# Scans with shifted dense rows and shared silu tables, an earlier spread of C, a router's logits moved up, and squares moved to GpSimd

## The reference, cut to what matters

```python
# grouped experts (layer 1, twice): 16 experts, the best 4 within 2 of 4 groups, two shared experts
scores = sigmoid(x @ router.T)          # the rest of the routing is left out
h = silu(x @ gate.T) * (x @ up.T)
y = combine(scores) * (h @ down.T)
...
# scans (layer 2): block a is one selective scan, block b is the difference of two
h_t = exp(delta_t * A) * h_(t-1) + (delta_t * u_t) * B_t     # 16 states for each of 256 inner features
y_t = sum over states of h_t * C_t, + D * u_t                # times silu(z), then a projection
delta = softplus(...);  u = silu(conv(...))
# the dense rows between and behind them (layer 2, twice)
h = silu(x @ w1 * s1) * (x @ w2 * s2)
h = gelu(h @ h1 * sh1);  h = gelu(h @ h2 * sh2);  y = h @ w3 * s3
...
# soft experts (layer 3, twice): 64 experts of 32 slots
D = softmax over slots (logits);  C = softmax over experts (logits)
X = tanh(layernorm(sum over tokens of D * x))
Y = X @ expert_w + expert_b
y = sum over experts and slots of C * Y
```

## Time and profile before

| | us |
|---|---|
| median of 3 runs | 3169.46 (3167.76 to 3170.31) |
| the profiled execution | 3163.47, of which its span 3161.8 |
| TensorE busy with products (PE) | 2879.4 (91% of the span) |
| TensorE loading weights (PEld, beside PE) | 1663.5 (53%) |
| VectorE busy (DVE) | 2187.7 (69%) |
| ScalarE busy (ACT) | 1641.4 (52%) |
| GpSimd busy (POOL) | 1119.3 (35%) |

### The profile page before, as it was taken

The page is one execution under the profiler, slowest core; times in us unless marked ns, Lnnn a source line. Parts: engine busy times, 40 slices in busy tenths (PEclk is TensorE's granted clock), DMA queues, the critical chain, the costliest instruction groups (busy, mean ns, idle before and its releaser), DMA issues. The chain is left out here.

```text
span 3161.8 us, 59104 instructions
## 1 busy us (share of the span) xinstructions
PE 2879.4 (91%) x22949; PEld 1663.5 (53%) x22949; DVE 2187.7 (69%) x4853; ACT 1641.4 (52%) x3287; POOL 1119.3 (35%) x534
## 2 busy tenths in 40 slices
PE   7888899998999999998968998898889899998999
PEld 3333344443899999643434544444454344574547
DVE  6777735556677777667588877877861559936991
ACT  3554543443333333326367776776753556725762
POOL 1111130002100000100088887877840209922990
PEclk8999999999555555699979999999999999999999
DMA  5344323022000000030532332222302001250225
GB/s 160 91 104 106 92 83 112 10 87 90 4 4 4 4 4 4 2 110 1 179 124 87 83 100 86 83 83 81 96 27 89 16 1 80 93 200 1 93 93 200
DMA packets 113494, 234.36 MB, mean 74 GB/s; under 512 B 13760, under 2 KB 50752, under 8 KB 104768
## 3 DMA queue, kind: packets, MB, share of 16 engines
q1 hardware_dynamic: 113216, 230.59, 22.7%
HBM read 185.71 MB, written 44.83 MB: 73 GB/s over the span
## 5 line engine op out<-in xcount | busy, mean ns | idle before, releaser
L2724 DVE TENSOR_TENSOR_SCAN s_hh<-psum,s_dbu 128x512 f32<-128x512 f32 x384 | 447.1, 1207 | 65.1 <-ACT psum L2337 62.4
L1447 PE MATMUL psum<-h_ring,h_parts 128*128 128x4 f16 x12264 | 478.3, 168 | 0.8 <-DVE h_ring L1590 0.6
L2594 POOL TENSOR_TENSOR s_dbu<-s_du,s_bb 128x1024 f32<-128x1024 f32 x191 | 446.7, 2362 | 60.9 <-DVE s_hh L2724 49.9
L1447 PEld LDWEIGHTS psum<-h_ring,h_parts 128*128 128x128 f16 x12264 | 430.5, 106 | 48.1 <-DVE h_ring L1590 0.8
L1509 ACT ACTIVATE h_now<-psum 128x16 f32<-128x16 f32 x1024 | 187.3, 183 | 325.5 <-PE psum L1447 319.0
L2337 ACT ACTIVATE psum<-s_delta,s_decay 128x512 f32<-128x512 f32 x384 | 256.4, 686 | 105.5 <-DVE s_hh L2724 103.4
L2229 PEld LDWEIGHTS psum<-w_c,s_term 128*128 128x128 f32 x1536 | 196.5, 148 | 129.5 <-issue 114.1
L1590 DVE TENSOR_SCALAR h_ring<-h_now 128x16 f16<-128x16 f32 x1024 | 179.3, 175 | 115.5 <-ACT h_now L1509 4.7
L1000 POOL MEMSET r_weights<- 128x512 f32 x4 | 2.1, 524 | 720.7 <-POOLq L1399 512.0
L2229 PE MATMUL psum<-w_c,s_term 128*128 128x128 f32 x1536 | 227.5, 284 | 6.7 <-ACT s_y L2415 6.2
L1592 DVE SCALAR_TENSOR_TENSOR h_ring<-h_now,h_ring 128x16 f16<-128x16 f32 x1024 | 181.2, 177 | 35.2
(11 more groups left out here) (585 smaller groups left out, 6257.9 us busy)
## 6 DMA issues: line engine op xcount, KB each, us to landing
s_bb<-s_wide SPq DMA_DIRECT2D x192, 256.0 KB, 3.5
x_spill<-x_flip SPq DMA_DIRECT2D x28, 1024.0 KB, 3.8
f_share<-f_wide SPq DMA_DIRECT2D x208, 128.0 KB, 3.0
s_cc<-s_wide SPq DMA_DIRECT2D x60, 256.0 KB, 3.4
a_ks<-a_spread SPq DMA_DIRECT2D x96, 128.0 KB, 3.4
a_qs<-a_spread SPq DMA_DIRECT2D x96, 128.0 KB, 3.9
x_spare<-x_spill SPq DMA_DIRECT2D x4, 2048.0 KB, 10.5
x_raw<-x_spill SPq DMA_DIRECT2D x4, 2048.0 KB, 9.3
```

Of the source, the lines that this page charges most:

```text
L1447: mm = nc.tensor.matmul(here[:, cols], parts[:, part, GROUP * grp + p, :], ring[:, (i - 1) % RING, grp, cut, cols], start=False, stop=True ...
L2594: nc.gpsimd.tensor_tensor(dbu[:, s % D_RING], du[:, t % 2], both(bb[:, s % B_RING, :]), ALU.mult).then_inc(dbu_ready, 1)
L2724: nc.vector.tensor_tensor_scan(hh[:, s % 4, half, :], DECAYS[i % 3], dbu[:, s % D_RING, half, :], 0.0, ALU.mult, ALU.add).then_inc(scan_do ...
```

## The change

1. Scans. Chunks 2 to 5 of the dense rows begin three or four slots later (`DENSE_AT`), and their pauses stand so that they stay where they were in time. The squashes and the gelu bends move to odd slots (`squash_slot`, `bend_slot`): from 14 and 26 of a turn to 15 and 27, or 31 in turns 4 and 8. The gate's bend stays at place 13, one slot earlier for chunk 2. At the slots 59, 175 and 287 a squash and a gate's bend now share one slot, and between them the table of silu stays loaded: the squash leaves out its last load and the bend its first.
2. Scans, TensorE. C's spread for step s goes ahead of the second half of the term of step s-3.
3. Grouped experts, first pass only. The logits go from behind gate and up of item 0 to between the two. VectorE norms the fourth chunk ahead of the second cut of the weights, and GpSimd makes its second cut of the inputs only when all cuts of the weights are made.
4. Soft experts, both. The four squares go from ScalarE to GpSimd, as multiplications ahead of its last division; VectorE's last sum goes behind its four scalings.

```diff
@@ gated_experts, TensorE
                         three_products(bank[i % 2 * 2], 0, m, c).then_inc(gate_ready, 1)
+                        if cuts_first and i == 0:
+                            logits()
...
-                    if i == router.LOGITS_AT:
+                    if i == router.LOGITS_AT and not cuts_first:
                         logits()
@@ gated_experts, GpSimd
                 nc.gpsimd.memset(weights[:], 0.0).then_inc(cleared, 1)
+                if cuts_first:
+                    pool.wait_ge(lo_made, MATRICES)
                 cut_inputs(1)
@@ gated_experts, VectorE
                 norm.vector(dve, 2)
+                norm.vector(dve, 3)
                 if cuts_first:
                     make_cuts(1)
-                norm.vector(dve, 3)
@@ scans_and_dense
-    DENSE_AT = (46, 101, 160, 215, 270, 321)
-    PAUSES = ((25,), (2, 31), (41,), (48,), (), (6,))
+    DENSE_AT = (46, 101, 163, 219, 274, 325)
+    PAUSES = ((25,), (2, 31), (38,), (44,), (), (2,))
...
+    def squash_slot(t):
+
+        if prepares(t):
+            return SLOTS * t + (14 + late(t) if late(t) else 15)
+        return SLOTS * t + (31 if t in (4, 8) else 27) if gate_job(t) is not None else None
...
+    bend_slot = {place(d, o) // 2 * 2 + 1: (d, name) for d in range(HIDDEN) for name, o in (("h1", 33), ("h2", 46))}
+    bend_slot |= {place(d, 13) - (d == 2): (d, "gate") for d in range(HIDDEN)}
@@ scans_and_dense, TensorE
+                    if s < STEPS and by_vector(s):
+                        pick_c(s)
                     if s >= 3 and s != STEPS:
                         add_up(s - 3, 1)
...
-                    if s < STEPS and by_vector(s):
-                        pick_c(s)
@@ scans_and_dense, ScalarE
-                def squash(ju, jz):
+                def squash(ju, jz, bends_next):
...
-                    nc.scalar.preload_act_table_set("natural_log_exp_and_others")
+                    if not bends_next:
+                        nc.scalar.preload_act_table_set("natural_log_exp_and_others")
...
-                    nc.scalar.preload_act_table_set(table)
+                    if table:
+                        nc.scalar.preload_act_table_set(table)
...
+                    if SLOTS * t + s in bend_slot:
+                        d, name = bend_slot[SLOTS * t + s]
+                        if name == "gate":
+                            bend(d, name, high, ACT.Silu, ffn["s1"], gated, None if SLOTS * t + s == squash_slot(t) else "silu_and_others")
+                        else:
+                            bend(d, name, {"h1": high, "h2": low}[name], ACT.Gelu, ffn["s" + name], act_done, "gelu_and_others")
@@ soft_experts, ScalarE
-                    square(0)
-                    square(1)
                     for j in range(PARTS):
                         invert(j)
-                        if j + 2 < PARTS:
-                            square(j + 2)
@@ soft_experts, GpSimd
                     lower_across(TILES - 1)
+                    for j in range(PARTS):
+                        pool.wait_ge(centred, j + 1)
+                        nc.gpsimd.tensor_tensor(fixed_(rstd, j), fixed_(z, j), fixed_(z, j), ALU.mult).then_inc(squared, 1)
                     divide_across(TILES - 1)
@@ soft_experts, VectorE
-                    sum_across(TILES - 1)
                     for j in range(PARTS):
...
                         nc.vector.tensor_tensor(fixed_(z, j), fixed_(z, j), fixed_(rstd, j), ALU.mult).then_inc(scaled, 1)
+                    sum_across(TILES - 1)
```

More of the change, by code:

```diff
@@ L2426, in chain @@
                             keep_conv(j, int(at == 13))
-                        if at == 14:
-                            squash(j, None)
+                        if SLOTS * t + s == squash_slot(t):
+                            squash(j, None, SLOTS * t + s in bend_slot)
                         if at == 17:
@@ L2448, in chain @@
                             keep_gate(gate_job(t), int(s == 25))
-                        if s == 26:
-                            squash(conv_job(t), gate_job(t))
+                        if SLOTS * t + s == squash_slot(t):
+                            squash(conv_job(t), gate_job(t), SLOTS * t + s in bend_slot)
                     if ended_job(t) is not None and s == 6:
@@ L2484, in dense @@
                         keep_scaled(d, "gate", (o - 7) // 2, high, ffn["s1"])
-                    if o == 13:
-                        bend(d, "gate", high, ACT.Silu, ffn["s1"], gated, "silu_and_others")
                     if o in (24, 27, 30):
                         keep_scaled(d, "h1", (o - 24) // 3, high, ffn["sh1"])
-                    if o == 33:
-                        bend(d, "h1", high, ACT.Gelu, ffn["sh1"], act_done, "gelu_and_others")
                     if o in (37, 40, 43):
                         keep_scaled(d, "h2", (o - 37) // 3, low, ffn["sh2"])
-                    if o == 46:
-                        bend(d, "h2", low, ACT.Gelu, ffn["sh2"], act_done, "gelu_and_others")
                 def slot(t, s):
@@ L3470, in _ @@
                             keep(n + 1, 3)
-                    def square(j):
-                        act.wait_ge(centred, j + 1)
-                        nc.scalar.activation(fixed_(rstd, j), fixed_(z, j), ACT.Square).then_inc(squared, 1)
                     def invert(j):
```

## The result

The changed kernel takes 3143.48 us (median of 4 runs, 3138.31 to 3148.74) against 3168.61 of the kernel before (4 runs): a ratio of 0.9922, 95% interval 0.9909 to 0.9934, or 25.1 us less. Forecast were 3147.5, in 3130 to 3161, and faster with a chance of 0.87. The profiled execution took 3144.3 us, span 3142.6; the forecast for it was 3141.5.

A forecast was written before the change was run, and what follows sets the result against it. The prediction took the scans to be bound by VectorE with ScalarE in front and TensorE close behind; scans -16.5, router -5.5 and soft experts 0 made -22, from 3169.5 to 3147.5 us, range 3130 to 3161.

The forecast's parts named there:

- Pairs taken apart: Scans: separating ScalarE's adjacent sequences at slots 154/155, 248 and 302/303 saves 3.1, 5.0 and 3.5 us, together -11.6.
- the rule for what stays behind once a pair is apart: Scans: a ScalarE sequence of length L with n VectorE-formed terms in its cover stops VectorE about L - 1.8 - 1.1n us.
- Shared tables: Scans, slots 59, 175, 287: dropping two of four table loads each saves 2.3, 4.2 and 1.7 us, together -8.2.
- The other moved sequences: Scans: remaining moved ScalarE sequences, priced by the rule alone, gain or lose covering terms, together +1.5 us.
- The dense rows: Scans: rows shift by 3 or 4 slots with the same work and pauses, giving nothing of itself.
- more goes than the rule says: Scans rival: waits for TensorE inside sequences end too and spreads gain; scans -28, time 3136 us, chance 0.18.
- TensorE takes over: Scans rival: what ScalarE's stops lose comes back before the terms; scans -4, time 3160 us, chance 0.16.
- sharing brings nothing: Scans rival: shared sequences stop VectorE as long as two shorter ones; scans give 9.1, time 3155 us, chance 0.10.
- C's spread, 0: Scans, TensorE: spreading C ahead of the older term's second half gains nothing; bounds -8.7 and +15.7 us.
- The slower rival: Scans: the spread's wait holds the older half behind it; scans 15.7 us longer, time 3179.7 us, chance 0.06.
- The router, -5.5: First grouped experts: logits fill TensorE's wait before up, so the next gate comes earlier; -5.5 us, bounds -9 and -2.7.
- Soft experts, 0: Both soft layers: expert products come 1.3 us earlier, but the late sum delays division and flips; net 0.

The follow-up runs named there:

- Experiment 3: The changed kernel with both table loads put back at the three shared slots (six loads more): 3155.93 us, ratio 0.9958.
- experiment 1: The kernel before with only ScalarE's sequences, the dense rows and the shared tables changed; spread, router and soft experts left as before: 3142.06 us, ratio 0.9917.
- Experiment 6: The changed kernel with C's spread in its old place and thirteen squashes and gelu bends half a step earlier, on even slots: 3140.95 us, ratio 0.9919.
- experiment 7: The changed kernel with C's spread in its old place and the dense rows of chunks 2 to 5 at their old slots: 3157.00 us, ratio 0.9964.
- experiment 2: The kernel before with only C's spread moved ahead of the second half of the older term: 3170.22 us, ratio 1.0009.
- experiment 5: The changed kernel with C's spread in its old place and the soft experts' sum ahead of the scalings again, squares still on GpSimd: 3133.25 us, ratio 0.9897.
- experiment 8: The kernel before, unedited, run again for a second trace: 3170.89 us.

## Why the prediction was right, point by point

- **The bound.** Right: VectorE does the same work, and what the stage gave was its idle time. One reading in that paragraph was wrong: most of the 42.1 us before the terms (25.0) had no releaser, and TensorE ended 12.6.
- **Pairs taken apart, -11.6: too much.** By the idle time of VectorE behind them in the changed kernel, 154 and 155 gave 2.1 (4.85 to 0.57 + 2.17; 3.1 forecast). 248 gave 2.8 and not 5.0: softplus and bend apart leave 1.64, 0.65 and, before a term, 1.55 where one wait of 6.68 was. 302 and 303 gave 0.5 and not 3.5: they had cost 5.79 (2.75 and 3.04) and not the 4.85 of the other pair, and left 1.65, 2.13 and, before a term, 1.55. Some 5.4 in all. The step that failed is the rule for what stays behind once a pair is apart: it priced only the scan that waits for ScalarE, and in both places a wait before a term (1.55) came up beside it.
- **Shared tables, -8.2: right.** Slot 59 went from 5.99 (3.70, 1.80 and 0.49) to 3.67 (2.74 and 0.93), -2.3 as forecast; 175 from 8.5 to 4.1, -4.4 against -4.2. Slot 287 went from 3.5 to 0.9, -2.6 against -1.7. Experiment 3 makes the loads alone worth 10.6 in the scans, most of it by way of TensorE, which the forecast had counted at slot 59 only.
- **The other moved sequences, +1.5:** not settled. The wait of 1.60 behind the first moved one is gone, but in experiment 1 the taps behind it took 10.28 us where they had taken 8.55, and the first turn stayed at 63.3 us; 363 cost 1.8 of 2.2. Experiment 6 bears out the sum for thirteen sequences, and the rule for single ones not.
- **The dense rows, "nothing of itself": wrong, by some 5 us in turn 8 (experiment 7).** The scans' waits for ScalarE fell by 15.7 us. The sign in the forecast was a fall to about 42: it came to 46.7 in the changed kernel, and to 41.0 without the spread (experiment 1). Beyond that VectorE waited 6.5 us less for TensorE's products and 4.1 less before its terms, and for these the forecast had next to nothing. Two causes are shown: the rows' products no longer stand beside other work of TensorE's (turn 8), and TensorE waits less for ScalarE's shortened sequences (experiment 3, and slots 175 to 177 in experiment 7). How those 6.5 and 4.1 us divide between them, no run shows. So the stage gave 24.8 where 16.5 were forecast, within the bounds of 4 and 28. The rival "more goes than the rule says" had named such waits, at too high a price; "TensorE takes over" and "sharing brings nothing" fall.
- **C's spread, 0: right** (experiment 2), with the reason that the forecast gave: a stop that goes comes back elsewhere. The slower rival's point of decision was not reached, as the idle time before the terms fell from 42.1 to 38.0.
- **The router, -5.5: right in its stage** (-5.9, and -5.4 over all traces). The logits took a time between the two that were set, and the lower clock behind them lasted half as long as before. By the rule of the Trainium skill's TensorE: Matmul & The Clock Gate, section "What's actually happening", the logits behind one gate were expected at the lower clock and the term at -2.7; the trace shows the first 2.4 us of them at the full one (until 1331.0), so that reading was too pessimistic.
- **Soft experts, 0: right**, with the working: flips 0.18 us later behind the first mean product, and the second fetch late by 0.23. The four squares took 4.04 us, where 5.1 were reckoned. The gain was there to be had: it was the late sum that ate it (experiment 5).
- **The sum:** -22 forecast, -25.1 measured. Right in size, and in part by luck: two errors inside the scans cancel in part (the pairs too much, VectorE's waits for TensorE too little), and some of the gain that the traces show is lost in stages that the change does not touch. The two profiled executions differ by 19.2 us only.

The Trainium skill's ScalarE: Activation LUTs, section "What ACT_TABLE_LOAD costs", counts a drain beside each load. Here an activation followed the load at slot 175 within 0.01 us, and ScalarE's busy time in the scans fell by 9.5 us; the drain is not seen in either.

```profile
1924.16 1.28 ACT L2368 ACT_TABLE_LOAD   x1
1925.45 1.06 ACT L2371 ACTIVATE s_u<-s_u 128x1024 f32<-128x1024 f32 x1
```

## What to carry to other kernels

Where one engine is paced by another, an edit that lets it arrive earlier at the same stop gives nothing (the spread: 7.6 us gained before the terms, 7.3 lost before the scans); look for the edit that makes the stop itself shorter. When work is moved, price what every engine had beside it at the old place, and follow a late engine through every engine that reads from it: here ScalarE's loads stopped VectorE more by way of TensorE (9.1 of 10.6 us in experiment 3) than at the scans that the working had priced. When a run undoes a move, list what else goes with it: experiment 7 took back two shared tables with the shift, and cannot price the shift alone. And when a step is moved off one engine, ask at once who the next one in the chain is: the squares were worth 1.4 us a layer, and that only with the sum behind them back in its early place.

## What the runs showed of the hardware

Equal scan code took 757.4, 757.3 and 760.1 us in three executions, and 729.2, 729.3 and 733.0 in three others (experiment 8). Over the whole kernel executions differ by several us. Part of that is spells of TensorE at 1.2 GHz that come in one execution and not in another: the second grouped pass, untouched, took 96.1 us at a granted clock of 1.00 and 100.2 at 0.95, and the same first-layer experts 138.2 us at 0.98 in the kernel before and 141.5 at 0.95 in the changed one. It is not all: the scans of 757.3 and of 760.1 us were both granted 0.93, and where their difference comes from stays open. An edit worth 5 us cannot be judged on this kernel by the whole time alone; it was judged by its stage.
